# Softmax stage of a graph network: copies of the first late step in four parts, late numerators first

## The reference, cut to what matters

```python
w_m = (efeat @ W_msg + b_msg).reshape(E, in_f, -1)
w_a = (efeat @ W_attn + b_attn).reshape(E, in_f, -1)
h_src = feat[src][:, :, None]
e1 = w_m * h_src
e2 = w_a * h_src
seg_max = jax.ops.segment_max(e2, dst, num_segments=N)
ex = jnp.exp(e2 - seg_max[dst])
denom = jax.ops.segment_sum(ex, dst, num_segments=N)
attn = ex / denom[dst]
ft = jax.ops.segment_sum(e1 * attn, dst, num_segments=N)
return ft.sum(axis=1)
```

## Time and profile before

| | us |
|---|---|
| median of 3 runs | 9713.91 (9710.63 to 9717.96) |
| the profiled execution's own time | 9719.54 |
| its span, from the first to the last instruction | 9717.7 |
| mean granted TensorE clock over the span | 0.911 of full |

### The profile page before, as it was taken

The page is one execution under the profiler, slowest core; times in us unless marked ns, Lnnn a source line. Parts: engine busy times, 40 slices in busy tenths (PEclk is TensorE's granted clock), DMA queues, the critical chain, the costliest instruction groups (busy, mean ns, idle before and its releaser), DMA issues.

```text
span 9717.7 us, 129425 instructions
## 1 busy us (share of the span) xinstructions
PE 7811.0 (80%) x35487; PEld 4162.5 (43%) x35487; DVE 7305.6 (75%) x13006; ACT 3031.2 (31%) x12664; POOL 6877.6 (71%) x5177
## 2 busy tenths in 40 slices
PE   0799995999965888888888888845888985899994
PEld 0465553555532333333333333313555653455552
DVE  2566662555536999999999999986888885788884
ACT  0111111000005777777777777731000000000000
POOL 5688886788877766666666666636888886688887
PEclk6899996999987999999999999967999997899996
DMA  1344442233324777777777777765323231433332
GB/s 32 94 114 110 102 104 48 61 76 70 69 38 117 203 203 207 204 203 202 203 205 206 203 202 203 204 192 157 82 70 82 70 82 37 107 100 100 100 105 48
DMA packets 823092, 1218.47 MB, mean 125 GB/s; under 512 B 237316, under 2 KB 687320, under 8 KB 802209
## 3 DMA queue, kind: packets, MB, share of 16 engines
q1 hardware_dynamic: 574895, 999.46, 34.3%
q0 software_dynamic: 212624, 110.62, 9.8%
q10 hardware_dynamic: 35440, 106.85, 3.5%
HBM read 421.45 MB, written 788.86 MB: 125 GB/s over the span
## 4 chain that ended last, share of the span: by engine, by line
POOL 45%; PE 17%; ACT 16%; issue 13%; DVE 5%; DMA 2%; SPq 1%; DVEq 0%; ACTq 0%; POOLq 0%
POOL arena L594 45%; ACT arena L808 14%; PE PS L1152 5%; PE PS L1153 4%; PE PS L1121 2%; PE PS L985 2%; PE PS L1122 1%; ACT arena L849 1%; DVE arena L1912 1%; PE PS L1113 1%; PE PS L1115 1%; PE PS L1105 1%; ACT arena L827 1%; DVE arena L1736 1%; DMA arena<-d_lane 1%
## 5 line engine op out<-in xcount | busy, mean ns | idle before, releaser
L985 PE MATMUL PS<-arena,TB 128*128 128x500 bf16 (+1 forms) x16038 | 3546.8, 376 | 225.0 <-DVE TB L1650 179.3
L594 POOL DMA_INDIRECT arena<-d_feat,srci x1650 | 2127.3, 1289 | 1237.7 <-ACT arena L808 753.8
L985 PEld LDWEIGHTS PS<-arena,TB 128*128 128x128 bf16 x16038 | 1581.0, 100 | 1862.7 <-issue 217.7
L594 POOL DMA_INDIRECT arena<-d_h,srci x1485 | 1959.2, 1319 | 569.8 <-issue 451.1
L808 ACT ACTIVATE arena<-PS,arena 125x32 f32<-125x32 f32 x10560 | 2012.0, 445 | 354.9 <-PE PS L1105 323.8
L1435 DVE TENSOR_SCALAR arena<-arena,lane 128x2000 bf16<-128x2000 f16 (+2 forms) x1848 | 1228.6, 723 | 576.3 <-DMA arena<-d_lane 330.6
L594 POOL DMA_INDIRECT arena<-d_rel,irel x858 | 1208.7, 1409 | 313.0 <-issue 261.2
L594 POOL DMA_INDIRECT arena<-d_nn,srci x759 | 1069.2, 1409 | 295.0 <-issue 230.4
L1152 PE MATMUL PS<-arena,ident 125*125 125x512 f32 x1650 | 962.6, 666 | 312.1 <-DVE arena L1740 211.7
L1447 DVE SCALAR_TENSOR_TENSOR arena<-arena,lane,PS 128x500 f32<-128x500 f16 x891 | 632.2, 712 | 626.0 <-PE PS L988 534.3
L1153 PE MATMUL PS<-arena 125*125 125x512 f32 x1650 | 887.6, 621 | 0.0
(11 more groups left out here) (285 smaller groups left out, 7692.9 us busy)
## 6 DMA issues: line engine op xcount, KB each, us to landing
d_smax<-arena SPq DMA_DIRECT2D x165, 1120.0 KB
d_sums_low<-arena SPq DMA_DIRECT2D x330, 560.0 KB
d_sums_high<-arena SPq DMA_DIRECT2D x330, 560.0 KB
arena<-d_pick SPq DMA_DIRECT2D x66, 843.8 KB
d_x<-arena ACTq DMA_DIRECT2D x165, 241.7 KB
arena<-d_x SPq DMA_DIRECT2D x165, 241.7 KB
arena<-d_lane SPq DMA_DIRECT2D x66, 527.3 KB
d_rel<-arena SPq DMA_DIRECT2D x50, 669.4 KB
```

What stands on the lines that cost most here:

```text
L594: gp.indirect_dma_start(out=dst, out_offset=None, in_=table, in_offset=bass.IndirectOffsetOnAxis(ap=index, axis=0)).then_inc(S(sem), 16)
L985: pe.matmul(PS[:, acc_at(L, q):acc_at(L, q) + w], TB[:, part, g * LANES * F:(g + 1) * LANES * F], OH[L][i][:, g, at:at + w], start=g == 0 ...
```

## The change

It concerns the order within the softmax stage; the arithmetic and the number of instructions stay, apart from one wait less a block (row sum 6 no longer waits for a weigh).

- ScalarE: the 16 copies of late step 6 (of block b + 2) go in four parts of four, one behind each of exponentials 0 to 3, where before all 16 stood between exponentials 3 and 4. The first part waits for the late weigh of the block that used the buffer last, now that block's first weigh; the last part counts `soft_ap`.
- TensorE: the product of late step 6 goes from ahead of difference 4 to ahead of difference 0.
- VectorE: the late weigh (four steps, `weigh(o, z, AT, NA)`) goes from behind maximum 13 to behind maximum 1, the first of the older work. The weigh of steps 2 and 3 goes ahead of maximum 7, and row sums 1 and 2 each go behind one more maximum: maxima 7 and 8 now stand ahead of row sum 1, 9 and 10 ahead of row sum 2; row sums 3 and 4 and the weigh of steps 4 and 5 follow one place later.
- The counts that wait for weighs follow the new order.

```diff
--- before.py
+++ after.py
@@ -795,19 +795,21 @@
             for c, (lo, hi) in enumerate(TAIL):
                 root(f"ln2_{c}", lo, hi)
 
-            def scaled(b, s, k, t):
+            def scaled(b, s, k, t, lo=0, hi=F):
 
                 n = t - AT
-                act.wait_ge(S("soft_am"), NA * b + n + 1)
-                if n == 0:
+                if lo == 0:
+                    act.wait_ge(S("soft_am"), NA * b + n + 1)
+                if n == 0 and lo == 0:
                     act.wait_ge(S(f"soft_late_g{s}"), 16 * NA * (k + 1))
                     if not isinstance(b, int) or b >= 3:
-                        act.wait_ge(S("soft_num"), 4 * (b - 2))
+                        act.wait_ge(S("soft_num"), 4 * (b - 3) + 1)
                 bank = (4 + n % 2) * 512
-                for i in range(F):
+                for i in range(lo, hi):
                     ins = act.activation(PB[:, s, n, 2 * F * i:2 * F * (i + 1)], PS[0:P, bank + 2 * F * i:bank + 2 * F * (i + 1)],
                                          ACT.Copy, scale=GH[:, s, t, i:i + 1])
-                ins.then_inc(S("soft_ap"), 1)
+                if hi == F:
+                    ins.then_inc(S("soft_ap"), 1)
 
             def first_rows(b, s):
 
@@ -840,8 +842,6 @@
                 if left >= 1:
                     scaled(b + 1, (s + 1) % 3, k + (s == 2), AT + 3)
                 for n in range(6):
-                    if n == 4 and left >= 2:
-                        scaled(b + 2, (s + 2) % 3, k + (s >= 1), AT)
                     act.wait_ge(S("soft_diff"), 6 * b + n + 1)
                     bank = PS[0:P, (6 + n % 2) * 512:(7 + n % 2) * 512]
                     if n < 5:
@@ -850,6 +850,8 @@
                            .then_inc(S("soft_exp"), 1)
                     else:
                         act.activation(DC, bank[:, 0:CH], ACT.Exp, bias=KR[:, s, 0, 0:1]).then_inc(S("soft_exp"), 1)
+                    if n < 4 and left >= 2:
+                        scaled(b + 2, (s + 2) % 3, k + (s >= 1), AT, 4 * n, 4 * n + 4)
 
             act.wait_ge(S("h_soft"), 1)
             for t in range(AT, B1):
@@ -1108,7 +1110,7 @@
             def first_sum(b, s):
 
                 pe.wait_ge(S("soft_exp"), 6 * b + 6)
-                pe.wait_ge(S("soft_num"), 4 * b + 1)
+                pe.wait_ge(S("soft_num"), 4 * b + 2)
                 bank = PS[0:P, 3584:4096]
                 pe.matmul(bank, ident[0:P, 0:P], XD[:, s, 0, :], start=True, stop=False)
                 pe.wait_ge(S("soft_carry"), b + 1)
@@ -1133,7 +1135,7 @@
                     products(b + 1, ahead, k1, 1)
 
                 for n in range(6):
-                    if n == 4 and left >= 2:
+                    if n == 0 and left >= 2:
                         scalable(b + 2, (s + 2) % 3, k + (s >= 1), AT)
                     if n == 4 and left >= 1:
                         products(b + 1, ahead, k1, 2)
@@ -1773,8 +1775,8 @@
                     dve.wait_ge(S("soft_first"), b + 1)
                     last = PS[0:P, 3584:4096]
                 else:
-                    if t in (2, 4, 6):
-                        dve.wait_ge(S("soft_num"), 4 * b + t // 2 + 1)
+                    if t in (2, 4):
+                        dve.wait_ge(S("soft_num"), 4 * b + t // 2 + 2)
                     dve.wait_ge(S("soft_sum"), (B1 - 2) * b + t - 1)
                 v.scalar_tensor_tensor(to, last, KR[:, s, t, 1:2], to, ALU.mult, ALU.add).then_inc(S("soft_sum"), 1)
 
@@ -1787,6 +1789,7 @@
 
             def late_sums(b, s):
 
+                weigh(b, s, AT, NA)
                 weigh(b, s, 0, 2)
                 carry(b, s)
                 row_sum(b, s, 1)
@@ -1794,7 +1797,6 @@
                 row_sum(b, s, 2)
                 row_sum(b, s, 3)
                 weigh(b, s, 4, 2)
-                weigh(b, s, AT, NA)
                 for t in range(4, B1 - 1):
                     row_sum(b, s, t)
 
@@ -1817,6 +1819,7 @@
                 top(b, s, 0)
                 product(b, s, 1)
                 top(b, s, 1)
+                weigh(o, z, AT, NA)
                 top(b, s, 2)
                 product(b, s, 2)
                 top(b, s, 3)
@@ -1825,20 +1828,19 @@
                 top(b, s, 5)
                 carry(o, z)
                 top(b, s, 6)
+                weigh(o, z, 2, 2)
                 top(b, s, 7)
+                top(b, s, 8)
                 row_sum(o, z, 1)
-                top(b, s, 8)
-                weigh(o, z, 2, 2)
                 top(b, s, 9)
+                top(b, s, 10)
                 row_sum(o, z, 2)
-                top(b, s, 10)
+                top(b, s, 11)
                 row_sum(o, z, 3)
-                top(b, s, 11)
+                top(b, s, 12)
                 weigh(o, z, 4, 2)
-                top(b, s, 12)
+                top(b, s, 13)
                 row_sum(o, z, 4)
-                top(b, s, 13)
-                weigh(o, z, AT, NA)
                 top(b, s, 14)
                 row_sum(o, z, 5)
                 top(b, s, 15)
```

## The result

| | before | after |
|---|---|---|
| median of 5 runs each, run together | 9717.96 us (9710.63 to 9727.31) | 9769.29 us (9766.52 to 9784.04) |
| profiled execution, its span | 9719.54, 9717.7 | 9784.04, 9782.2 |
| mean granted clock over the span | 0.911 | 0.888 |
| mean distance of the 165 carries, last one left out | 20.56 us | 20.95 us |

The ratio is 1.0055, 95% interval 1.0041 to 1.0070: the change makes the kernel about 0.5% slower. The forecast was 9700 with a range up to 9720, so it was wrong, and on the wrong side. The profiled execution is the slowest of the five; it is 64.5 us longer than that of before, and 163 x (20.95 - 20.56) = 64 us of it are the softmax stage. What stands ahead of its first carry and behind its last differs by under 5 us.

The account below looks back on a forecast made before the run. VectorE with its wait and a ScalarE-TensorE ring were taken as equally long bounds, about 20.56 us a block. 163 x (20.56 - 20.48) = 13 us plus 1 us off 9719.5 gave 9705.5, median 5.6 lower: 9700, range 9662 to 9720.

Parts of the forecast that it names:

- The wait for the first sum: VectorE's wait for TensorE's sum of each block's first row (L1115): gone, worth 0.30 us a block, ends 0.22 and 0.38.
- VectorE's own period: VectorE's time per softmax block without that wait: 20.56 - 0.30 = 20.26 us.
- The ring at full clock: Chain of waits round ScalarE and TensorE, once a block: 19.1 us, 19.5 with starts after waits, below VectorE's 20.26.
- the 21.2 of the prediction: Length in us of the ScalarE and TensorE ring with half clock, costing 1.7, full on running matmuls.
- The half clock in nearly every block: TensorE's longer pauses bring a 3.4 us stretch at 1.2 of 2.4 GHz to nearly every block; mean stage clock 0.92.
- the pause ahead of difference 0: TensorE idle between the products and difference 0, which waits for late step 8's copies: 2.2 us, before 1.32.
- the two new pauses: TensorE's idle times ahead of the first sum, 1.7 us (before 0.1), and ahead of difference 0, 2.2 us (before 1.32).
- The feedback by the stores: A longer ring delays stores of the sums until VectorE waits, some 0.2 us a block; 1.3 us of delay free.
- a longer one slides it back into the pause, where it costs nothing: Half-clock stretches recur at 20.48 us; blocks longer than that move them off TensorE's differences into its pause, at no cost.
- The balance is a ring of 20.48: Block period in us settles there: 19.5 plus 1.0 of half-clock cost, about 2 of 3.4 us on running matmuls.
- Half clock twice a block: Rival, chance 0.10: both TensorE pauses followed by half clock, ring 20.85 us, 47 us slower, 9760 us.
- The full wait won: Rival, chance 0.33 (or most of it): ring stays below 20.26, VectorE bounds, 49 us gained, 9664 us.

Follow-up runs that it names:

- e4: Changed kernel with both TensorE pauses filled: product of early steps 2 and 3 made four times, four added matmuls ahead of the first sum; 9661.6 us, ratio 0.9938.
- e7: Changed kernel with the product of late step 6 behind difference 0 and four added matmuls ahead of the first sum; 9659.5 us, ratio 0.9944.
- e12: Changed kernel with late step 6's product behind difference 0 and the next block's early steps 0 and 1 product ahead of the first sum; 9661.7 us, ratio 0.9940.
- e6: Changed kernel with only the pause ahead of the first sum filled, by four added matmuls; 9770.5 us, ratio 1.0055.
- e5: Changed kernel with only the pause ahead of difference 0 filled, the product of early steps 2 and 3 made four times; 9675.2 us, ratio 0.9960.
- e9: Kernel before with one move alone: TensorE's product of late step 6 ahead of difference 0 instead of difference 4; 10057.3 us, ratio 1.0350.
- e10: Kernel before with the pause ahead of difference 0 filled, the product of early steps 2 and 3 made four times; 9724.7 us, ratio 1.0006.
- e11: Changed kernel with the pause ahead of difference 0 partly filled, the product of early steps 2 and 3 made twice; 9769.0 us, ratio 1.0055.
- e3: Changed kernel with one move: TensorE's product of late step 6 behind difference 0 instead of ahead of it; 9669.8 us, ratio 0.9946.
- e1: Kernel before with VectorE's new order alone, ScalarE and TensorE keeping their old order; 9698.0 us, ratio 0.9978.

## Why the prediction was wrong

**VectorE (right).** The wait for the first sum is gone and VectorE's own period is 20.21 us where nothing holds it (e4, e7, e12); predicted 20.26. The wait was worth 0.35, near the end of 0.38.

**The ring at full clock (right as far as shown).** I summed 19.1, and 19.5 with the starts after waits. No run shows the bare number, since VectorE bounds at 20.21; the turn of 20.90 less the 1.74 of its slow difference is 19.16. The 0.4 that I added for starts after waits is not there: from the product of late step 6 to that of late step 7 TensorE waits for nothing. A stretch wholly on the differences makes 20.90, not the 21.2 of the prediction.

**The half clock in nearly every block (right).** 163 stretches, clock 0.91, forecast 0.92; the pause ahead of difference 0 is 2.32 us, forecast 2.2. Of the two new pauses that one carries the loss (e6); with it filled, the other still brings 35 stretches and 0.1 us a block (e5 against e4).

**The feedback by the stores (right in kind).** 68.0 us, 96 times, and last sum for another 32.3 us; forecast some 0.2 us a block, measured (68.0 + 32.3) / 163 = 0.6.

**The step that failed.** It is this one: "a longer one slides it back into the pause, where it costs nothing. The balance is a ring of 20.48". The slide is there, and the recurrence of 20.48 too. And the ring comes close to the balance: with the stretch 0.5 us ahead of the pause's end it is 20.54, 1.4 above 19.16. I had the cost as 1.0 above 19.5, with 1.4 us of the stretch in the pause. But there is no balance to rest in. From 0.55 us ahead the stretch does not become cheaper, it doubles. The price is a block of 22.17 and a restart of the slide at 20.90. Why it doubles there is not shown. The mean is 20.95 in place of 20.48: 163 x 0.47 = 77 us, and 9700 + 77 = 9777, near the 9769 measured. The earlier trace rows had a hint that I read over: in the kernel before, a run of stretches ended at place 10.4, 0.5 us ahead of difference 0, though the pause had begun 1.3 us ahead of it. And the one stretch of that trace that starts deeper in a pause, 1.1 us ahead of difference 0 in the last block, is its only one of 6.8 us; both halves of it are at half clock:

```profile
6379.30:6382.70 3.40, 2.33 (x3) 1.16 (x4) 3.40 (x7) 0.00 (x0) 0.00 (x0) 0.50 0.74 230
6382.70:6386.10 3.40, 3.40 (x5) 1.32 (x4) 3.40 (x7) 0.60 (x1) 0.00 (x0) 0.50 0.72 226
```

The 64 deep stretches of e9 say the same.

**The rivals.** "Half clock twice a block" gave the nearest time, 9760 at a chance of 0.10, with a mechanism that isn't the one, and with a ring of 20.85 that was its 22.1 less an overlap of 1.25 us read from no row, so that the nearness is luck: no block has two stretches, a seventh of them have one of double length, and filling the first pause gives nothing back (e6). "The full wait won", 9664, is what e4, e7 and e12 measure, once the clock is held or difference 0 is early. The Trainium skill, TensorE: Matmul & The Clock Gate, A second HAM failure mode, says that frequent short idles between groups of matmuls make the clock swing. The trace agrees, with 163 stretches and a period 0.4 us longer than before and 0.7 longer than in e4, and e4 shows it by its reverse; I had given it too little weight beside a balance that I had worked out from one side only.

## What to carry to other kernels

A matmul queue that waits a little longer can lose more than the wait: before moving work ahead of a group that waits, ask how long TensorE will then be idle and whether what follows has slack at half clock. If the half clock can't be avoided, start the dependent group earlier, so that it costs nothing: here moving one product behind the first difference turned +0.5% into -0.5%. And where a feedback is argued to settle at a balance, check both ends of the slide in the trace of before: here its one stretch that began deep in a pause was not hidden there but twice as long.

## What the runs showed of the hardware that was not expected

- The half clock comes in stretches of 3.4 or 6.8 us. After one of 3.4 the next starts 20.48 us later, after one of 6.8 it is 23.89 (the kernel after, 161 of 162 distances). One that starts up to 0.54 us ahead of the end of the pause of 2.32 us lasts 3.4 us there, one that starts 0.55 to 0.65 us ahead, or 0.6 to 1.8 in e9, lasts 6.8.
- Adding ten matmuls a block made the changed kernel some 110 us faster (e4); in the kernel before, six more changed nothing (e10).
- One product moved from ahead of difference 4 to ahead of difference 0 cost 336 us when ScalarE's copies stayed in one piece (e9): 22.5 us a block, with 96 stretches of double length.
- A pause of 1.8 us ahead of the differences brought 62 stretches (e12), one of 1.89 150 (e11), one of 2.32 163, all in 165 blocks; one of 1.34 (e3) none over the differences but in the last block. The length of this pause alone does not decide: with 1.32 us there and 0.67 ahead of it the kernel before had 56, and e1, with up to 1.34 us there, had none.
